# One program for attention and experts: twelve expert blocks begin before the attention part has drained

## The reference

```python
x = x + W_out(attention(q = W_q(layernorm(x)), k = W_k(ctx), v = W_v(ctx)))
n = layernorm(x)
logits = n @ Wr + br;  topk_val, topk_idx = top_k(logits, 2);  scores = softmax(topk_val)
h = n @ W1[e] + b1[e];  a, g = split(h);  out_e = (silu(a) * g) @ W2[e] + b2[e]
x = x + sum over the two experts of scores * out_e
```

## Time and profile before

| | us |
|---|---|
| median of three runs | 1299.19 |
| the profiled execution, whole | 1298.25 |
| its span, first to last instruction | 1296.4 |
| PE busy in the span | 1178.3 |
| DVE busy | 999.1 |
| ACT busy | 807.0 |
| POOL busy | 620.9 |

### The profile page before, as it was taken

The page is one execution under the profiler, slowest core; times in us unless marked ns, Lnnn a source line. Parts: engine busy times, 40 slices in busy tenths (PEclk is TensorE's granted clock), DMA queues, the critical chain, the costliest instruction groups (busy, mean ns, idle before and its releaser), DMA issues. The chain is left out here.

```text
span 1296.4 us, 38380 instructions
## 1 busy us (share of the span) xinstructions
PE 1178.3 (91%) x12538; PEld 1042.2 (80%) x12539; DVE 999.1 (77%) x2926; ACT 807.0 (62%) x1640; POOL 620.9 (48%) x728
## 2 busy tenths in 40 slices
PE   5899999999999999740499999999999999999986
PEld 4677777777777777530499999999999999999986
DVE  5788888888888887734478888888888888887763
ACT  5676666666666666412376766766667666676552
POOL 5346666666666665542034344344443444432333
PEclk9999999999999999855699999999999999999998
DMA  5122333233333222216767777777777677776553
GB/s 173 41 82 89 98 96 96 98 98 103 103 102 103 94 71 70 70 60 204 252 162 180 192 163 181 178 170 191 165 180 183 165 191 167 180 184 156 149 151 37
DMA packets 106527, 175.81 MB, mean 136 GB/s; under 512 B 13040, under 2 KB 81840, under 8 KB 106288
## 3 DMA queue, kind: packets, MB, share of 16 engines
q1 hardware_dynamic: 77376, 135.47, 32.3%
q0 software_dynamic: 26592, 36.46, 17.1%
q10 hardware_dynamic: 2448, 2.44, 0.6%
HBM read 126.21 MB, written 47.60 MB: 134 GB/s over the span
## 5 line engine op out<-in xcount | busy, mean ns | idle before, releaser
L1306 POOL DMA_INDIRECT out_rows<-y_gated,block_tokens x142 | 263.7, 1857 | 433.5 <-DVE y_gated L1278 333.2
L1064 PE MATMUL bank<-block_T_hi,w_hi 128*128 128x256 f32 x1136 | 328.2, 289 | 10.6 <-DVE block_T_lo L1252 10.6
L1066 PE MATMUL bank<-block_T_hi,w_lo 128*128 128x256 f32 x1136 | 321.3, 283 | 0.0
L1065 PE MATMUL bank<-block_T_lo,w_hi 128*128 128x256 f32 x1136 | 321.2, 283 | 0.0
L1064 PEld LDWEIGHTS bank<-block_T_hi,w_hi 128*128 128x128 f32 x1136 | 215.7, 190 | 12.6 <-DVE block_T_lo L1252 7.9
L1065 PEld LDWEIGHTS bank<-block_T_lo,w_hi 128*128 128x128 f32 x1136 | 216.0, 190 | 0.0
L1066 PEld LDWEIGHTS bank<-block_T_hi,w_lo 128*128 128x128 f32 x1136 | 215.7, 190 | 0.0
L491 ACT ACTIVATE probs_T<-bank 128x512 f32<-128x512 f32 x256 | 132.2, 603 | 98.3 <-PE bank L322 98.3
L1160 ACT ACTIVATE act_hi<-act 128x512 fp32r<-128x512 f32 x142 | 89.8, 632 | 150.7 <-DVE act L1262 150.7
L1262 DVE SCALAR_TENSOR_TENSOR act<-bank,block_b,silu_a 128x256 f32<-128x256 f32 x284 | 124.3, 480 | 75.1 <-ACT silu_a L1141 45.5
L599 DVE TENSOR_REDUCE row_max<-bank 128x4 f32<-128x512 f32 x256 | 158.9, 683 | 22.4 <-PE bank L303 22.4
(11 more groups left out here) (151 smaller groups left out, 2504.2 us busy)
## 6 DMA issues: line engine op xcount, KB each, us to landing
w_raw<-in_L_ffn_W SPq DMA_DIRECT2D x71, 1024.0 KB
block_rows<-routed_rows SPq DMA_DIRECT2D x71, 272.0 KB, 3.3
x_in<-in_x SPq DMA_DIRECT2D x64, 128.0 KB, 2.4
ctx_T<-in_ctx SPq DMA_DIRECT2D x16, 512.0 KB, 3.9
x_res<-in_x SPq DMA_DIRECT2D x64, 128.0 KB, 2.7
out_rows<-x SPq DMA_DIRECT2D x64, 128.0 KB, 2.3
w_raw<-in_L_ffn_W SPq DMA_DIRECT2D x8, 512.0 KB, 7.8
out_rows<-y_gated,block_tokens POOLq DMA_INDIRECT x142, 4.4
```

The lines of the kernel that those rows point to most:

```text
L1064: mm(dst, w1h[:, k, c, at:at + P], xh[:, k, c, :], start=(c == 0), stop=False)
L1065: mm(dst, w1h[:, k, c, at:at + P], xl[:, k, c, :], start=False, stop=False)
L1066: last = mm(dst, w1l[:, k, c, at:at + P], xh[:, k, c, :], start=False, stop=(c == KC - 1))
L1306: nc.gpsimd.indirect_dma_start(out=out[:, :], out_offset=bass.IndirectOffsetOnAxis(ap=tk[:, u % U, t:t + 1], axis=0), in_=yg[:, u % 2, t, ...
```

## The change

There is one Block now, and each engine's list runs from the attention slots straight into the expert blocks. The tables for the first M = 12 blocks are made from the counts of the first 48 tiles: only whole blocks of rows that are already scattered are taken, in order of the experts. The other 59 blocks come from the final counts, with these twelve left out. Buffers of the expert part lie over buffers of attention that are no longer used by then (`overlaid`), which is why the second W1 buffer is loaded only after slot 64. In detail:

- slots 54 to 57 on DVE: four pieces of the early table; slot 58: the idle rows' tile;
- slots 56 to 59 on ACT: eight loads of W2 are issued; slots 60 to 63: ACT and DVE split two experts of W2 in each;
- slot 62 on SP: W1 and rows of block 0, rows of block 1; slot 63 on ACT and DVE: W1 of block 0 is split (`w1_hi`, `w1_lo`);
- slots 65 to 69: each is followed on every engine by one expert block, 0 to 4. On PE the transposes and the output projection, then ranks and logits, stand in front of the block's products;
- after block 4 on DVE: the late tables; after blocks 5 to 8 on ACT: two stores of idle rows each; SP waits for these and for all scatters before it loads block 12;
- on POOL the adds of blocks 0, 1, 2 stand in front of slots 67, 68, 69.

```diff
+    EARLY = NB * 3 // 4
+    M = 12
...
         @block.tensor
+            def expert_slot(i, u):
+                up_half(i, u, 0)
+                if has(i, u + 1):
+                    rows_T(i, u + 1)
+                up_half(i, u, 1)
+                if has(i, u - 1):
+                    if isinstance(i, int) and blk(i, u) == 1:
+                        pe.wait_ge(s_w2l, E)
+                        pe.wait_ge(s_x2, NB)
+                    down(i, u - 1, expert(i, u - 1))
...
-            run(before, slot)
+            before()
+            for t in range(NB + 1):
+                slot(t)
...
+            for k in range(GB + 1):
+                squares_and_out(NB + 1 + k)
+                ranks_and_logits(NB + 1 + k)
+                expert_slot(k // U, k % U)
+            turns(pe, expert_slot, GB + 1)
...
         @block.scalar
+            def prepare(t):
+                if 56 <= t < 60:
...
+                    for e in range(2 * (t - 56), 2 * (t - 55)):
+                        act.dma_start(w2l[:, e * FC * D:(e + 1) * FC * D].bitcast(F32).rearrange("p (c n) -> p c n", c=FC),
+                                      w2[e].rearrange("(c p) n -> p c n", p=P)).then_inc(s_w2[e], 16)
+                if 60 <= t < 64:
...
+                        nc.scalar.activation(w2h[:, e * FC * D:(e + 1) * FC * D],
+                                             w2l[:, e * FC * D:(e + 1) * FC * D].bitcast(F32), ACT.Copy).then_inc(s_w2h, 1)
+                if t == NB - 1:
+                    w1_hi(0, 0)
+                if t == NB:
+                    x_hi(0, 0)
...
+            for k in range(GB + 1):
+                slot(NB + 1 + k)
+                expert_slot(k // U, k % U)
+            for k in range(GB + 1, GB + 1 + E // 2):
+                expert_slot(k // U, k % U)
+                if k == GB + 1:
+                    act.wait_ge(s_tab, 2)
+                idle_rows(range(2 * (k - GB - 1), 2 * (k - GB)))
+            turns(act, expert_slot, GB + 1 + E // 2)
...
         @block.vector
+            for k in range(GB + 1):
+                last_sums(NB + 1 + k)
+                last_routing(NB + 1 + k)
+                expert_slot(k // U, k % U)
+            late_tables()
+            turns(dve, expert_slot, GB + 1)
...
         @block.gpsimd
+            slot(NB + 1)
+            slot(NB + 2)
+            for i in range(2):
+                pool.wait_ge(s_x2d[i], 16 * (NB // 2))
+            pool.wait_ge(s_dum, 32)
+            for k in range(GB - 1):
+                expert_slot(k // U, k % U)
+                slot(NB + 3 + k)
+            turns(pool, expert_slot, GB - 1)
```

More of the change, by code:

```diff
@@ L92, in pairs, with blk, has, upto @@
         return (t // 2 + 1) * per
+    def blk(i, u):
+        return i * U + u
+    def has(i, u):
+        return not isinstance(i, int) or 0 <= i * U + u < NT
+    def upto(i, u, per=1, done=None):
+        return i * (U * per) + (u * per + (per if done is None else done))
+    def upto2(i, u):
+        return i * (U // 2 * 16) + (u // 2 + 1) * 16
+    def turns(eng, slot, begun):
+        for b in range(begun, M):
+            slot(b // U, b % U)
+        with eng.Fori(M // U, NTURN - 1) as i:
+            for u in range(U):
+                slot(i, u)
+        for u in range(NT - U * (NTURN - 1)):
+            slot(NTURN - 1, u)
@@ L189, in attention @@
+        s_meta = sem("block_meta_read"); s_bT = sem("block_T_done"); s_bh = sem("block_hi_done"); s_bl = sem("block_lo_done")
+        s_a = sem("up_a_done"); s_g = sem("up_g_done"); s_sa = sem("silu_done"); s_ac = sem("act_done")
+        s_ah = sem("act_hi_done"); s_al = sem("act_lo_done"); s_y = sem("down_done"); s_yg = sem("y_gated_done")
+        s_add = sem("rows_added"); s_turn = sem("add_turns")
         block = ctx.enter_context(nc.Block())
[L191 to L195 removed]
@@ L434, in slot, with rows_T @@
                     pv(t - 1, 3)
-            run(before, slot)
+            def rows_T(i, u):
+                pe.wait_ge(s_ld[u % 2], upto2(i, u))
+                if has(i, u - 1):
+                    pe.wait_ge(s_bl, upto(i, u - 1))
+                for c in range(KC):
+                    for t in range(ET):
+                        last = nc.tensor.transpose(bank[5][:, c * EB + t * P:c * EB + (t + 1) * P],
+                                                   xb[:, u % 2, t, c * P:(c + 1) * P], ident)
+                last.then_inc(s_bT, 1)
@@ new lines, in up @@
+            def up(i, u, bk, half, side):
+                k = u % 2
+                for m in range(HM):
+                    at = side * F + (HM * half + m) * P
+                    dst = bk[:, m * EB:(m + 1) * EB]
+                    for c in range(KC):
+                        mm(dst, w1h[k][:, c, at:at + P], xh[:, k, c, :], start=(c == 0), stop=False)
+                        mm(dst, w1h[k][:, c, at:at + P], xl[:, k, c, :], start=False, stop=False)
+                        last = mm(dst, w1l[k][:, c, at:at + P], xh[:, k, c, :], start=False, stop=(c == KC - 1))
+                return last
@@ new lines, in idle_tile, with expert_slot @@
+            def idle_tile():
+                V.memset(pad, 0.0).then_inc(s_padz, 1)
+                dve.wait_ge(s_padz, 1)
+                for t in range(ET):
+                    last = V.tensor_scalar(pad[:, t, TOK:TOK + 1].bitcast(I32), consts[:, C_P:C_P + 1], float(T + t * P), None, ALU.add)
+                last.then_inc(s_pad, 1)
+            def expert_slot(i, u):
+                first = isinstance(i, int) and blk(i, u) == 0
+                if has(i, u + 1) and not first:
+                    w1_lo(i, u + 1)
+                mult(i, u, 0)
+                if has(i, u + 1):
+                    meta(i, u + 1)
+                act_lo(i, u, 0)
+                mult(i, u, 1)
+                if has(i, u + 1):
+                    x_lo(i, u + 1)
+                act_lo(i, u, 1)
+                if first:
+                    w1_lo(i, u + 1)
+                if has(i, u - 1):
+                    gate(i, u - 1)
@@ L809, in _ @@
+            before()
+            for t in range(NB + 1):
+                slot(t)
+                prepare(t)
+            for k in range(GB + 1):
+                last_sums(NB + 1 + k)
[3 more added lines that the diff above has]
+            turns(dve, expert_slot, GB + 1)
+            gate(NTURN - 1, NT - U * (NTURN - 1) - 1)
         @block.gpsimd
```

843 lines of the change are left out of this document (445 added, 398 removed).

## The result

The changed kernel takes **1341.47 us** (median of 4, 1340.5 to 1344.62) against 1300.4 for the kernel before, timed beside it: ratio 1.032, 95% interval 1.029 to 1.0349. It is slower. The forecast was 1262 (1239 to 1287), so even the range is missed. What came is the rival "a lock of the adds", which I had priced at 1319 us and given a chance of 0.09.

A forecast was written before the change was run, and what follows sets the result against it. The prediction took PE to bound each part, but not the seam between them. Its terms, -57.1 + 3.4 + 1.3 + 1.4 + 1.6 + 5.9 + 6.4 = -37.1 us, gave 1262 us, range 1239 to 1287.

The forecast's parts named there:

- a lock of the adds: Rival: from block 3 on, late adds keep some 53 blocks at 10.05 us, not 8.98; +57, 1319 us, chance 0.09.
- the late tables hold the blocks up by 6 us just then: Argument against the lock: tables behind block 4 delay blocks 6 us, and POOL is idle again before block 4's adds.
- a lag of about 3 us kept into block 5: Condition said to decide whether the late adds on POOL lock the expert loop.
- three signs of being wrong: Forecast wrong if mid-stretch blocks take 10 us, block 0 starts after 585, or slots 60 to 64 grow over 15 us.
- Up to slot 60: Term for early tables on DVE (0.8 us) and W2 load issues on ACT (1.2): +2.0 us (0 to 7).
- Slots 60 to 64: Term for W2 and W1 conversions on ACT and DVE, less DVE's waits: +9.2 us (0 to 18.3).
- Block 0's first product: PE's start of the expert blocks, forecast at 573.8 instead of 630.9: -57.1 us, the gain.
- Blocks 0 to 12: Terms behind block 0's start: +3.4, +1.3, +1.4, +1.6, late tables +5.9, idle rows +6.4 us; 8.98 us a block otherwise.
- The late tables: Term for 18 table steps, 6.1 us, in front of DVE's part of block 5: +5.9 us (2 to 7).
- the idle rows at 1.6 us a block: Term for two stores on ACT in front of each of blocks 6 to 9: +6.4 us in all (0 to 9.4).
- The tail: End of the kernel, taken as unchanged, with some 8 us lost there as before.
- The function table: Slot 68: two ACT table loads counted at 1.28 us each without the skill's drain, within a +1.4 us term (0 to 3).

The follow-up runs named there:

- e11: Kernel before with POOL held up once by 5 memsets ahead of block 3's adds, 1.1 us late: 1278.39 us.
- e12: Kernel before with POOL held up once by 6 memsets ahead of block 3's adds, 2.2 us late: 1351.52 us.
- e1: Changed kernel with its last eight scatters issued two behind the adds of each of blocks 3 to 6: 1239.72 us, ratio 0.9697.
- e4: Changed kernel with block_tokens copied in two steps, moving DVE's wait for adds from mid-slot to just ahead of y_gated: 1238.98 us, ratio 0.9705.
- e2: Kernel before with POOL alone held up once by 17 memsets ahead of block 3's adds: 1353.52 us.
- e13: e6 with DVE's late tables spread over blocks 5 to 8 and b1's rows loaded in slot 52 instead of 56: 1219.41 us, ratio 0.9527.
- e6: e4 with ACT converting W2 in slots 60 to 62 and DVE subtracting each group one slot later: 1227.04 us, ratio 0.9627.
- e7: Kernel before with only the two-step token copy of e4: 1266.43 us, ratio 0.9917.
- e3: Changed kernel with W1 loads from block 2 on cut to a quarter of the bytes: 1240.33 us.
- e8: Kernel before with POOL held up once by 7 memsets ahead of block 3's adds, 3.2 us late: 1345.15 us.

## Why the prediction was wrong

**The step that failed** is the one that kept the lock at 0.09: "the late tables hold the blocks up by 6 us just then, and by my times POOL is idle again before the adds of block 4". I had block 3's adds 7 us late; they were ten late: the ten scatters took 14.0 us and not 12.7 (637.71 to 651.71), behind a second add of 2.61 us. POOL was idle again at 655.49, before block 4's gated result (656.66), as I had said; but it then waited until 664.23 for block 3's adds to land, over 10 us behind the start of the second. I had asked when POOL is free, and not when its last transfer has landed. More to the point, I had the place of decision wrong: "a lag of about 3 us kept into block 5". The trace of before had one lag that locked, and I took it for the threshold:

```profile
1157.38 2.28 POOL L1306 DMA_INDIRECT out_rows<-y_gated,block_tokens  x1 [4.86 <-DVE y_gated L1278]
1162.15 1.55 POOL L1306 DMA_INDIRECT out_rows<-y_gated,block_tokens  x1 [2.50 <-issue]
1169.27 1.55 POOL L1306 DMA_INDIRECT out_rows<-y_gated,block_tokens  x1 [5.56 <-DMA out_rows<-y_gated,block_tokens]
```

1169.27 - (1157.38 + 8.98) is a lag of 2.9 us. It bounds the point from above only; e11 and e12 put it between 1.1 and 2.2. Two of my own three signs of being wrong named this and the late seam: blocks of 10 us in mid-stretch (10.13), and a start of block 0 after 585 (586.53). And the six microseconds of tables came to nothing as a cover: once a load shares the flight of the second add, a pair needs longer than a block. In size the rival was short by 22 us (1319 against 1341): 6.2 of these are the three blocks between 664.23 and 700.80 us, which took 12.19 us each beside the idle-row stores, (12.19 - 10.13) x 3; another 12.7 are the late seam, next; the 3.6 left are about what a period of 10.13 in place of 10.05 makes over 50 blocks. That the idle-row stores stretched those three blocks is read from their times alone (655.33 to 691.19 on ACT's queue), not tested.

**The sum without the lock came out right by errors that cancelled.** e1 and e4 have the change without the lock of block 3: ratio 0.970 to before, where the forecast was 1262 / 1299.19 = 0.971. That is luck: in e4 some 13 us too little up to block 0 (43.5 gained against e2's 608.07, where I had 57.1) stand against 6.3 too much in blocks 0 to 12 and the 8 us of the tail.

- *Up to slot 60*, forecast +2.0. Slot 60 starts at 525.09; before, 7.80 us ahead of slot 61, at 517.89: +7.2. The early tables and ACT's W2 loads cost nearly nothing (slot 57 starts at 494.76 against 494.50). The 7 us are PE's wait for b1's rows, a transfer that the change moves to just in front of its reader. I had no term for it; the wait itself is 4.54 us, and e13 got 6.3 us back by moving the load.
- *Slots 60 to 64*, forecast +9.2. The last probabilities product ends at 582.2 against 558.6, 23.6 in all, so 16.4 here. I had counted DVE's and ACT's conversions as if they ran side by side and set DVE's waits off against them. In the order as written DVE's subtraction stands behind ACT's copy in the same slot, so the two add up and the wait for ACT comes on top. e6 took 12 to 13 us off by that alone. By my own criterion, "if slots 60 to 64 grow by over 15 us", the forecast was wrong.
- *Block 0's first product*, forecast 573.8: 586.53, the sum of these two and 0.3 us.
- *Blocks 0 to 12*: read in e4, which has no lock, by DVE's copies of the tokens, one a slot. From slot 0 to slot 1 13.9 us (forecast 15.4), slots 1 to 4 11.0, 10.2 and 9.8 (10.3, 10.4, 10.6), slot 4 to 5 14.7 with the tables (14.9), the four slots with idle rows 39.1 (42.3), and the two behind them 16.8 in place of 18.0. Together 6.3 us less than forecast. The late tables were right to 0.2 us; the idle rows at 1.6 us a block were twice too dear: I had taken half of the 4.70 us of four stores, and two stores here take 1.46 to 1.52 us of ACT's queue (e1).
- *The tail*: the forecast kept the 8 us lost at the end; e4 does not lose them, and e7 prices them at 10.7. e1 keeps a short lock there, in its last four blocks or so.

From block 0's first product to the end e4 takes 1235.9 - 564.54 = 671.4 us, the changed kernel 752.2. The 81 us between are the lock, its part at the kernel's end included.

**The rule on ordering.** I had read the Trainium skill, page DMA: Bandwidth & Descriptors, section Queues, rings and completion order, as support for the lock: an increment lands only after that DMA engine's earlier writes, from whichever queue. Runs agree as far as they go: 4.2 us beside 256 KB (e3), 7.0 in the lock beside 1024 KB (e8). But in the lock most loads are issued 0.25 us behind the second add and not ahead of it, so the load's writes would have to come first all the same, which no trace shows. That it is this order and not shared bandwidth is not shown either; no run tells the two apart.

**The function table.** ACT in slot 68, the two changes of table between blocks 2 and 3:

```profile
620.51 1.28 ACT L756 ACT_TABLE_LOAD   x1
621.81 0.21 ACT L756 ACTIVATE gate_exp<-gate_diff 128x4 f32<-128x4 f32 x1
...
623.93 1.28 ACT L800 ACT_TABLE_LOAD   x1
625.22 0.84 ACT L800 ACTIVATE silu_a<-bank,block_b 128x256 f32<-128x256 f32 x2
```

Each load takes 1.28 us and the next activation follows within 0.02; the instructions ahead of the loads end at 620.50 and 623.91, so nothing is lost before them either. The drain of 1.38 us that the Trainium skill gives (page ScalarE: Activation LUTs, section What ACT_TABLE_LOAD costs) does not show.

What stays open: why POOL has a gap of 2.5 us (before) or 3.4 us (after) just ahead of the second add of one late pair, the 242nd, 248th or 256th of its 270 scatters and adds in all sixteen traces, which starts the lock at the kernel's end; and whether e1's one long execution was such a gap come early.

## What to carry to other kernels

If a loop holds a state in which an engine waits for its own last transfer, even for a few turns at its end, ask what puts it there and whether it gets out by itself; then a one-time delay of 2 us can be worth the whole rest of the loop (75 us here), and not 2 us. Look which engine waits for that transfer in the middle of its list and move that wait to where it must stand, before moving the work that causes the delay: one copy of two columns was worth as much as the order of all scatters, and it holds against the next delay too. When work of two engines is put into one slot, write down which of them reads what the other writes in that slot; such pairs cost their sum on the path, and a lag of one slot between them took most of the wait away here (e6).

## What the runs showed of the hardware

- An indirect add of 128 rows lands in 4.2 us in the median when a 1024 KB load is issued 2.6 to 3.4 us behind the second of a pair (e1), and in 7.0 when it is issued some 0.3 us behind (e8); with 256 KB it lands in 4.2 (e3). One microsecond of lag decides which of the two a whole run gets (e11, e12).
- One hold of POOL of 6.6 us (e12, 2.2 us of it beyond its idle time) cost 75 us, one of 5.6 us cost 2.
- The kernel before took 1300 us in the first timing and 1276 to 1280 in the four later ones, and the 22 us lie ahead of its expert loop (block 0's first product at 630.93 and, in e2, at 608.07); a block in step takes 8.98 us in both (e11 for the later ones). Why is not shown.
- A load of ACT's function table takes 1.28 us, with 0.02 us or less lost before and behind it (changed kernel, slot 68).
